# A decoder layer on one core: routing work of VectorE split over two steps, two orders of units exchanged

## The reference

```
x = layernorm(x + attention(x))            # 16 heads of 64: softmax(q k^T / 8) v, then @ Wo + bo
x = layernorm(x + mlstm(x, ctx, ctx))      # 4 heads of 64, gates by cumsum of log_sigmoid and a running max
x = layernorm(x + moe(x))                  # norm, router softmax over 8 experts, the best 2 of them, F = 1024
```

## Time and profile before

| | us |
|---|---|
| median of 3 runs (lowest, highest) | 843.74 (843.56, 845.28) |
| time of the profiled execution | 843.9 |
| its span, first to last instruction | 842.1 |
| TensorE busy | 734.7 (87%) |
| VectorE busy | 472.6 (56%) |
| ScalarE busy | 330.7 (39%) |
| GpSimd busy | 238.2 (28%) |

### The profile page before, as it was taken

The page is one execution under the profiler, slowest core; times in us unless marked ns, Lnnn a source line. Parts: engine busy times, 40 slices in busy tenths (PEclk is TensorE's granted clock), DMA queues, the critical chain, the costliest instruction groups (busy, mean ns, idle before and its releaser), DMA issues.

```text
span 842.1 us, 15192 instructions
## 1 busy us (share of the span) xinstructions
PE 734.7 (87%) x5072; PEld 628.2 (75%) x5073; DVE 472.6 (56%) x1079; ACT 330.7 (39%) x989; POOL 238.2 (28%) x193
## 2 busy tenths in 40 slices
PE   4798999998979979799679989999999999998762
PEld 4687787877868868588668878888888888786320
DVE  4334444665855667647678844555555555555354
ACT  4575666655655646546442202222222222221011
POOL 2200010101303104022145456076077000600672
PEclk9899999998989989989685899999999999999655
DMA  8266674001001010020142245145135211210242
GB/s 310 62 218 227 202 255 157 2 13 55 10 26 51 14 38 26 2 63 2 57 156 76 88 140 155 39 162 168 37 119 170 78 37 37 63 33 20 82 145 79
DMA packets 62509, 77.40 MB, mean 92 GB/s; under 512 B 5836, under 2 KB 54520, under 8 KB 62456
## 3 DMA queue, kind: packets, MB, share of 16 engines
q1 hardware_dynamic: 53832, 47.29, 17.4%
q0 software_dynamic: 8608, 29.37, 10.9%
q10 hardware_dynamic: 16, 0.01, 0.0%
HBM read 45.04 MB, written 31.62 MB: 91 GB/s over the span
## 4 chain that ended last, share of the span: by engine, by line
PE 63%; DVE 13%; ACT 9%; POOL 6%; issue 6%; DMA 2%; another core or an unknown queue 0%; POOLq 0%; SPq 0%; DVEq 0%; ACTq 0%
PE bank L954 13%; PE bank L707 8%; PE bank L709 6%; PE bank L708 6%; ACT arena L1061 5%; PE bank L924 4%; PE bank L926 4%; PE bank L925 4%; PE bank L934 4%; PE bank L864 3%; PE bank L827 3%; POOL arena L697 3%; POOL xg_dram L632 1%; ACT arena L1034 1%; PE bank L876 1%
## 5 line engine op out<-in xcount | busy, mean ns | idle before, releaser
L954 PE MATMUL bank<-w_ring,hidT_hi 128*128 x320 | 121.2, 412 | 3.3 <-DVE hidT_lo L1575 3.3
L1179 ACT ACTIVATE hidT_hi<-bank 128x512 fp32r<-128x512 f32 x80 | 43.5, 595 | 176.2 <-PE bank L934 176.2
L1061 ACT ACTIVATE arena<-bank,negmx 128x128 f32<-128x128 f32 x256 | 90.8, 375 | 3.4 <-DVE negmx L1216 2.7
L632 POOL DMA_INDIRECT xg_dram<-arena,slot x32 | 33.8, 1055 | 181.2 <-DVE slot L1415 173.5
L954 PE MATMUL bank<-w_ring,hidT_lo 128*128 x320 | 84.1, 283 | 0.0
L1548 DVE TENSOR_TENSOR arena<-bank,b_rep 128x512 f32<-128x512 f32 x80 | 55.3, 691 | 40.9 <-PE bank L926 40.5
L1554 DVE TENSOR_REDUCE work<-bank 128x256 f32<-128x512 f32 x40 | 27.7, 692 | 81.0 <-PE bank L954 81.0
L954 PEld LDWEIGHTS bank<-w_ring,hidT_hi 128*128 128x128 f32 x320 | 60.8, 190 | 15.2 <-issue 3.9
L924 PE MATMUL bank<-w_ring,xgT_hi 128*128 x160 | 67.4, 421 | 4.5 <-DVE xgT_lo L1567 2.8
L926 PE MATMUL bank<-w_ring,xgT_lo 128*128 x160 | 63.8, 399 | 0.0
L925 PE MATMUL bank<-w_ring,xgT_hi 128*128 x160 | 62.9, 393 | 0.0
(11 more groups left out here) (243 smaller groups left out, 1882.7 us busy)
## 6 DMA issues: line engine op xcount, KB each, us to landing
xg_dram<-zeros SPq DMA_DIRECT2D x9, 2176.0 KB, 9.3
w_raw<-in_L_ffn_W_dram POOLq DMA_DIRECT2D x16, 1024.0 KB, 6.3
work<-xg_dram SPq DMA_DIRECT2D x40, 128.0 KB, 2.1
y_dram<-work SPq DMA_DIRECT2D x40, 128.0 KB, 1.7
b_rep<-in_L_ffn_b_dram POOLq DMA_DIRECT2D x8, 512.0 KB
work<-gmax_dram SPq DMA_DIRECT2D x14, 256.0 KB, 3.6
arena<-in_x_dram SPq DMA_DIRECT2D x8, 256.0 KB, 2.7
xres<-in_x_dram SPq DMA_DIRECT2D x1, 2048.0 KB, 15.2
```

The costliest lines, as they stand in the source:

```text
L954: last = pe.matmul(o, l, r, start=c == 0 and l is both[0], stop=c == FC - 1 and l is both[0])
L1061: last = nc.scalar.activation(probs[:, n % 2, h * S:(h + 1) * S], ps_score[:, h * S:(h + 1) * S], ACT.Exp, bias=negmx[:, n % 2, h:h + 1], ...
```

## The change

VectorE's `choose` is cut in two. `first_choice` finds the best expert (7 instructions) and stays at s = 1; `second_choice` finds the second best and all that follows (12 instructions) and goes to s = 2, ahead of `weights_of`. `head_sums` goes behind `weights_of` at s = 2. `find_slots` goes from s = 2, behind `weights_of`, to s = 3, ahead of `add_heads`. In the drain both halves still run one after the other.

GpSimd's `scatter` goes from s = 2 to s = 3, behind `head_norm` and ahead of `both_norms`; in pair 7 it so also falls behind the loads of the expert's weights.

ScalarE's `choice_exp` goes ahead of the copy of the transposed weights at s = 1.

TensorE: at s = 1 v(i, 0, 1) runs ahead of G (the gates are computed one unit later), at s = 2 k(i+1, 1) ahead of R, and at s = 3 k(i+1, 2) ahead of w(i, 0, 1). ScalarE's copies follow from the same lists. In the drain 29 empty matmuls are added ahead of units, and 15 at its end.

```
@@ fillers @@
             if s == 1:
                 return (of("T", i - 2) + of("L", i - 3) + of("X", i - 1) + of("x", i + 1) + of("v", i, 1, 0),
-                        of("G", i - 1) + of("v", i, 0, 1) + of("v", i, 1, 1))
+                        of("v", i, 0, 1) + of("G", i - 1) + of("v", i, 1, 1))
             if s == 2:
                 return (of("U", i - 2, 0) + of("q", i + 1, 0) + of("U", i - 2, 1) + of("k", i + 1, 0),
-                        of("q", i + 1, 1) + of("R", i - 3) + of("k", i + 1, 1))
+                        of("q", i + 1, 1) + of("k", i + 1, 1) + of("R", i - 3))
             return (of("v", i + 1, 0, 0) + of("S", i - 1) + of("q", i + 1, 2) + of("w", i, 0, 0),
-                    of("w", i, 0, 1) + of("k", i + 1, 2))
+                    of("k", i + 1, 2) + of("w", i, 0, 1))
@@ gpsimd @@
-                    if s == 2 and i >= 3:
-                        scatter(i - 3)
                     if s == 2 and i >= 2:
                         head_norm(i - 2)
+                    if s == 3 and i >= 3:
+                        scatter(i - 3)
@@ tensor @@
-            pauses = {("N", A): 6, ("U", Z, 0): 22, ("R", Y): 16, ("N", Z): 30, ("R", Z): 16}
+            pauses = {("N", A): 10, ("T", Y): 4, ("L", A): 6, ("R", A): 3, ("U", Z, 0): 22, ("R", Y): 20, ("N", Z): 34,
+                      ("R", Z): 20}
             for un in DRAIN:
                 fill(pauses.get(un, 0))
                 run([un])
-            fill(40)
+            fill(55)
@@ scalar @@
+                    if s == 1 and i >= 3:
+                        choice_exp(i - 3)
                     act.wait_ge(pT_done, n + 1)
                     nc.scalar.copy(pT, ps_pT).then_inc(pT_copied, 1)
                     copies(after[:1])
                     if n + 1 < STEPS * PAIRS:
                         exponentials(n + 1, 1)
-                    if s == 1 and i >= 3:
-                        choice_exp(i - 3)
@@ vector @@
+            def first_choice(p):
+
+                dve.wait_ge(route_exp_out, p + 1)
+                dve.tensor_reduce(tot, ex, AX.X, ALU.add).then_inc(tot_ready, 1)
+                pick(p, 0)
+                dve.wait_ge(tot_ready, p + 1)
+                chain.link(dve.scalar_tensor_tensor(ex, hot[:, 0, :, :], -2.0, ex, ALU.mult, ALU.add))
+
+            def pick(p, k):
+                pair = slice(2 * p, 2 * p + 2)
+                chain.link(dve.tensor_reduce(best[:, k, :], ex, AX.X, ALU.max))
+                chain.link(dve.tensor_tensor(is_top, ex, over_e(best[:, k, :]), ALU.is_equal))
+                chain.link(dve.tensor_tensor(is_top, is_top, over_b(em8[:, :]), ALU.mult))
+                chain.link(dve.tensor_reduce(idx[:, k, pair], is_top, AX.X, ALU.min))
+                chain.link(dve.tensor_tensor(hot[:, k, :, :], over_b(em8[:, :]), over_e(idx[:, k, pair]), ALU.is_equal))
+
+            def second_choice(p):
+
+                pair = slice(2 * p, 2 * p + 2)
+                pick(p, 1)
@@ vector, the loop @@
                     if s == 1 and i >= 3:
-                        choose(i - 3)
+                        first_choice(i - 3)
                     if s == 2 and i >= 1:
                         gate_sums(i - 1)
-                    if s == 2 and i >= 2:
-                        head_sums(i - 2)
+                    if s == 2 and i >= 3:
+                        second_choice(i - 3)
+                    if s == 3 and i >= 3:
+                        find_slots(i - 3)
                     if s == 3 and i >= 2:
                         add_heads(i - 2)
                     if n + 1 < STEPS * PAIRS:
@@
                     if s == 1 and i >= 1:
                         read_gates(i - 1)
-                    if s == 2 and i >= 3:
-                        find_slots(i - 3)
+                    if s == 2 and i >= 2:
+                        head_sums(i - 2)
```

More of the change, by code:

```diff
@@ L1375, in logits_in @@
                 dve.tensor_tensor(logit, logit, over_e(top), ALU.subtract).then_inc(route_exp_in, 1)
-            def choose(p):
-                pair = slice(2 * p, 2 * p + 2)
+            def first_choice(p):
                 dve.wait_ge(route_exp_out, p + 1)
                 dve.tensor_reduce(tot, ex, AX.X, ALU.add).then_inc(tot_ready, 1)
[L1382 to L1391, removed]
+                pick(p, 0)
[11 more added lines that the diff above has]
+                pick(p, 1)
                 chain.link(dve.tensor_tensor(chosen, hot[:, 0, :, :], hot[:, 1, :, :], ALU.add))
@@ L1401, in choose @@
                 chain.link(dve.tensor_tensor(wgt[:, pair, :], of_hot[:, 0, :, :], of_hot[:, 1, :, :], ALU.add))
+            def choose(p):
+                first_choice(p)
+                second_choice(p)
             def find_slots(p):
```

## The result

| | before | changed |
|---|---|---|
| median of 4 runs, us | 844.36 | 796.99 |
| lowest, highest | 843.56, 845.28 | 795.39, 799.31 |
| ratio, 95% interval | | 0.9455 (0.9434 to 0.9476) |
| span of the profiled execution | 842.1 | 796.3 |

The time fell by 5.2 to 5.7%; the forecast was 796.5. A ratio is given as the middle of its interval. The quotient of the two medians is 0.9439, so ratios that differ by 0.002 are not told apart. The busy time by stretch shows where: pair 1, pair 2, pairs 3 to 6, pair 7 until VectorE's last reading of w, and from there to the experts' first matmul. The columns are those of the earlier trace rows.

What follows compares the result with a forecast made beforehand. TensorE was taken to bound the loop, with one hole a pair made by VectorE's order. 17.0 + 1.9 + 15.4 + 8.0 + 6.3 - 0.9 = 47.7 off the 842.1 span gave 794.4, plus 1.8: 796.2, say 796.5; range 790 to 812.

Steps and rivals of the forecast that it cites:

- The bound and the chain: In the loop TensorE is the bound, with one hole a pair: U's copy waits on a chain over three engines.
- 17.0 for U's wait: TensorE's wait for U's second half at s = 2, pairs 2 to 6, goes: gain 17.0 us in all.
- 1.9 for k: TensorE's waits for k's buffer at s = 2, 3.4 us in all, shrink to 0.3 each: gain 1.9 us.
- 15.4 for the half clock: Without the long wait TensorE's half clock goes in pairs 2 to 6: gain 15.4 us, its last term least certain.
- 13.7 for pairs 3 to 6: Clock at 1.00 in pairs 3 to 6: four times 3.4 us, gain 13.7.
- Pair 2's 1.7: Pair 2's 3.4 us at half clock goes as its short waits shrink: gain 1.7 us.
- The clock rival: Short waits among U and k keep the clock falling: 1.7 us in five pairs, 8.5, so 805 us; chance 0.14.
- the rival of VectorE's queue: head_sums ahead of the maxima makes w(i, 0, 0) or the scores wait: up to 17.7 us, so 814; chance 0.08.
- 8.0 for k ahead of w: At s = 3 k's earlier copy removes the 1.15 us wait ahead of the next scores in seven pairs: gain 8.0.
- 6.3 in pair 7: VectorE's last reading of w in pair 7 comes earlier, at 36.6 instead of 42.9: gain 6.3 us, bounds 4.2 and 7.2.
- The scatter lock: Rival: VectorE's port lock stretches pair 7's four scatter DMAs by up to 1.55 us each, 6.2, so 803; chance 0.04.
- 0.9 lost by the empty matmuls: Added empty matmuls in the drain delay the experts but avoid half clock there: loss 0.9 us, bounds 0.6 and 3.2.

Runs made afterwards that it cites:

- the run with one round: The changed kernel with choose whole at s = 1 (all 19 instructions), the rest as changed: 795.77 us, ratio to before 0.9462.
- fewer empty matmuls: The changed kernel with 16 empty matmuls ahead of R(Y), 25 ahead of N(Z), 15 ahead of R(Z), 43 at the end: 793.49 us, ratio to before 0.9439.
- the version that the runs point to: The kernel before with v, choice_exp and k(i+1, 2) moved, head_norm ahead of scatter at s = 2, and fewer empty matmuls: 791.67 us, ratio 0.9411.

## Why the prediction was right

**The bound and the chain.** Right, step by step: a stall for U behind soft_gates, read_gates, weights_of, choose and choice_exp. Taking a link earlier moved the wait by somewhat more than was reckoned (2.1 left with v ahead, against 2.4 to 2.7; 0.5 with choice_exp ahead, against 0.8). What I had not seen is that the links overlap. With v and choice_exp both moved, choose's 3.68 us fit into the 3.7 us until the exponentials are done. The part that gives the change its name was costed at nothing lost, rightly, but the text let it look like part of the cure; the run with one round shows that it is not.

**17.0 for U's wait, 1.9 for k.** Both as forecast: no wait for U, 0.3 for each k.

**15.4 for the half clock.** The 13.7 for pairs 3 to 6 was too large: in 6.8 us at 0.50 TensorE was busy for 6.02 only, third column of the second of the earlier trace rows, so 3.0 a pair and 12.0. The busy time fell by 12.8. That is the whole of the missing 0.9 in pairs 3 to 6. Pair 2's 1.7 came. The clock rival did not, in pairs 2 to 6, nor did the rival of VectorE's queue: w waits for find_slots in pair 7 alone.

**8.0 for k ahead of w.** The mechanism holds, all seven waits are gone. In pair 1 a stretch of 3.4 us at half clock, which was not there before, took most of its gain back: the pair took 43.67, and 42.5 in the two kernels with this exchange whose profile shows no such stretch (fewer empty matmuls, and the version that the runs point to). The run with this edit alone shows a condition that the forecast had without naming it: in the pairs with routing it needs head_norm early.

**6.3 in pair 7.** It came to 7.25, next to the bound of 7.2. second_choice held TensorE for 2.92 (forecast 3), find_slots for 1.2 instead of 3, since R and the sums ahead of it ran at half clock and used the time. w was read at 35.7 on the pair's clock, the value forecast for full clock. That is partly luck: the clock was at 0.50 for 10.2 us of the pair all the same, the case for which the forecast had 38.7. It cost nothing since VectorE's own queue set the reading: L1358 ran until 385.08, the reading began at 385.11.

**The scatter lock.** First of a scatter beside add_heads in pair 5, on GpSimd:

```profile
287.63 1.44 POOL L632 DMA_INDIRECT xg_dram<-arena,slot  x1 [1.03 <-DVE slot L1425]
289.37 1.05 POOL L632 DMA_INDIRECT xg_dram<-arena,slot  x1 [0.30 <-issue]
290.73 0.96 POOL L632 DMA_INDIRECT xg_dram<-arena,slot  x1 [0.30 <-issue]
```

It takes 1.44 us, against 0.96 for the last of the four, and 1.06 for the first of them in pair 5 of the kernel before; and it has slack. In pair 7 scatter ran behind add_heads' wide operations and none took over 1.05. By the Trainium skill, SBUF — State Buffer, section "SBUF: two separate sides", the loser of the port pair stands still until the other's instruction ends; the trace agrees in kind: L1325, the operation of VectorE that was under way, lasted 0.69 and had 0.50 to run when the scatter began, while the one in the earlier trace rows lasts 2.29. The next one (L1327, also two operands in SBUF) ran beside the rest of the scatter, so the trace does not show the lock in full.

**0.9 lost by the empty matmuls.** This term failed in size at both ends. The part up to the experts grew by 4.5, not 2.6: I had the 2.3 of the last 55 nearly right (about 2: from their start to the transposes of the first rows it is 12.4 us, and 10.35 before), but put those ahead of N(Z) among the waits that they fill, and they made N(Z) 2.2 late. And what follows gave 2.7 back, not 1.7. From the experts' first matmul to their last it was 3.2: the stretch at half clock at their start went, as forecast, and so did a second one near their end, which the forecast did not have. In the kernel before:

```profile
768.58 0.49 PE L954 MATMUL bank<-w_ring,hidT_hi 128*128 x1 [2.12 <-DVE hidT_lo L1575]
```

```profile
769.70:773.10 3.40, 3.40 (x13) 2.83 (x12) 0.00 (x0) 0.00 (x0) 0.00 (x0) 0.51 0.00 0
```

The changed kernel has the same wait, and the clock stays at 1.00 behind it:

```profile
723.76 0.49 PE L955 MATMUL bank<-w_ring,hidT_hi 128*128 x1 [2.14 <-DVE hidT_lo L1587]
```

Why it fell in the one and not in the other stays open. What follows the experts took 0.6 more. So the second error takes back half of the first, and those of pairs 1 and 7 cancel: a sum off by 1.9 in the span hides single terms off by 1 to 2. That the forecast of 796.5 is only 0.5 from the median is luck beyond that, since the execution whose span it was summed for took 798.1, the second longest of the four.

## What to carry to other kernels

When a stall hangs on a chain over several queues, list for each link what it waits for once the others are moved: the slack that one edit opens may already hold the work that the next edit would cut up. A small instruction whose input is long ready but which stands behind a long group in an in-order queue is the first thing to move. Empty matmuls that keep the clock up are to be fitted to the wait that they fill, and fitted again when anything ahead of them changes. Here leaving them all out took the same time (0.945 against 0.9455).

## What the runs showed of the hardware

The length of the half clock followed the length of the wait ahead of it: in pairs 3 to 6, behind 4.15 us of idle 6.8 us at 0.50 in all four, behind 2.1 us 3.4 us in all four, behind 0.5 and 0.9 us 3.4 us in one pair of four, behind 0.3 none. With scatter ahead of head_norm it was 6.8 us behind 4.79 us and 3.4 us behind each of 3.84, 3.93 and 3.95. Beside this it varies without a change in the program: up to the drain the changed kernel and the one with fewer empty matmuls are the same, but pair 1 had 3.4 us at 0.50 in the one (clock 0.96 in the stretch shown first above) and none in the other. Of the nine kernels with k ahead of w(i, 0, 1), seven profiles have this stretch in pair 1 and two have none; of the five without that exchange none has it.
